# A step of the feed forward's norm one turn sooner: the last part of a four-layer gated transformer on one core

## The chip, the cores and the metric

One Trainium2 chip, one core of it. The metric is the device time of one execution in microseconds; the kernel before took 4783.49 us, the median of three runs (4782.34 to 4784.24).

## The reference

`x` holds 4 batches of 512 tokens with 256 features. Four layers of gated cross attention and feed forward follow each other, and the feed forward of the last layer is a transformer of its own, six deep. All that concerns us is inside it:

```python
def ffn_layer(x, g, bln, W1, b1, W2, b2):
    mu = x.mean(-1, keepdims=True)
    var = ((x - mu) ** 2).mean(-1, keepdims=True)
    xn = (x - mu) / jnp.sqrt(var + 1e-05) * g + bln
    hg = xn @ W1 + b1
    a, gate = jnp.split(hg, 2, -1)
    return a * jax.nn.gelu(gate, approximate=False) @ W2 + b2
for i in range(DEPTH):      # 6
    x = attn_layer(shift_tokens(x), Wqkv[i], q_scale[i], k_scale[i], Wo[i]) + x
    x = ffn_layer(shift_tokens(x), ln_g[i], ln_b[i], W1[i], b1[i], W2[i], b2[i]) + x
```

`attn_layer` is a local attention over windows of 64 tokens, 16 heads of 64 features. `shift_tokens` takes the second half of the features from the token before.

## The kernel before

The first part of the kernel (up to about 2124 us, where L1634 first runs) does everything but those six layers and isn't touched. The last part (`last_part`, L1276) works on transposed data, features in the partitions, in plain fp32 kept exact by splitting: each operand is a high part and a remainder (`xs_hi`, `xs_lo` and so on), and each product is three matmuls.

The order of the work is written out by hand. `last_order` (L1214) gives each stage of each unit a **turn**, sorts the stages of a turn by rank, and returns one list; every engine walks through the same list and issues its own share of each stage, in that order. A unit is a depth `d`, a quarter of the heads `g` and a batch `b`; it takes four turns, one per 128 tokens, so a depth has 64 turns and all six have 384. Turn numbers below are those inside a depth, 0 to 63, and batch 2's and 3's later steps fall in the next depth's first turns. In each turn, in this order:

- "sc": TensorE adds the window mask (L1511) and the scores (L1516); VectorE takes the row maxima (L1648) and combines them with the norms (L1652).
- "pv": TensorE multiplies with the values (L1535); ScalarE writes `att_hi` (L1777), VectorE the remainder (L1663).
- "tr": TensorE transposes queries and keys (L1501); ScalarE copies them out (L1752, L1757).
- "rot": POOL adds the two halves of the rotary product (L1818), takes the norm (L1820, L1822) and scales the keys (L1825); VectorE sums the squares for it (L1642).
- "dv", "ex": VectorE divides (L1657, L1659); ScalarE takes the exponentials (L1764).
- "pt": TensorE transposes the probabilities (L1525); ScalarE copies them out (L1770).
- "wx", in two of four turns: VectorE adds the output projection to the residual (L1670).
- then the feed forward's stages that have this turn, and "xs", the splitting of the next input (ScalarE L1735, POOL L1809).
- "qkv": TensorE projects (L1493, twelve matmuls); VectorE makes the rotary products (L1634, L1635, L1636); ScalarE copies the values (L1742) and squares (L1745), which frees the bank of queries and keys.
- "wo", in two of four turns: twelve matmuls of the output projection (L1449).
- "lq": a piece of weights: SyncE loads it, VectorE rounds it (L1618), POOL takes the remainder (L1814).

The feed forward of one batch, batches 0 and 2 ("even") from turn 32 of their half, batches 1 and 3 ("odd") from turn 49, has these steps:

- "fo": POOL adds the two halves of the features (L1830) into the buffer `n0`.
- "fa": TensorE multiplies with a matrix of 1/256 for the mean (L1556, two matmuls for the profile); VectorE subtracts it (L1676, twice) into `c0` and `c1`.
- "fq": ScalarE squares them (L1782, twice) into `n0` and `n1`; POOL adds (L1833).
- "fb": TensorE sums over the features (L1561); VectorE adds epsilon (L1680); POOL raises to the power -1/2 (L1836).
- "fy": TensorE spreads the result over the partitions (L1569); VectorE multiplies (L1685, twice).
- "fc": ScalarE adds the offset and rounds to `xn_hi` (L1790, twice).
- "fd": VectorE makes the remainder `xn_lo` (L1692, twice). The first gate product waits for it.
- "hg", three times: gate products (L1449, twelve matmuls) and ScalarE's gelu (L1798). "ha" and "hm", three times: linear products, VectorE's product of both (L1702), its rounding (L1709, L1712), POOL's remainder (L1842). The last "ha" and "hm" of a batch are in turn 50 (even) and 34 (odd, counted from the next half's start); so they fall one or two turns behind the next batch's "fo".
- "fw" and "fx": second product (L1449, L1596, L1597) in three parts, and VectorE's addition to the residual (L1717).

Memory is handed out by `plan` (L84) from the same list, when the program is built: a free slot is taken from the head of a queue and a freed one put at its end, so that the stage that opens a slot waits for the signal that freed it. Two of these queues matter here. `one` (L1360) deals out six PSUM banks. "qkv" takes two (freed by `sq_act`, that is L1745, and by L1742), "hg" two, and "fa", "fb", "fy", "tr", "pt", "pv" one each. `work_at` (L1402) deals out the nine buffers of `lwork`: "qkv" opens three (`sq`, `t1`, `t2`), "rot" frees `sq` and `t2` (the latter by POOL's L1825), "tr" three turns later frees `t1`; "fo" opens `n0`, "fa" `c0` and `c1`, "fq" `n1`; "fb" frees the two `n`, "fd" the two `c`; "hg" opens two for the gates, "hm" frees them (by POOL's L1842, the last by VectorE's L1712). VectorE waits for the buffers of `t1` and `t2` ahead of L1634.

```python
def plan(order, slots, opens, closes):
    free, held, got, turns = [(s, None) for s in slots], {}, {}, {}
    for p in order.parts:
        for key in opens(p):
            slot, before = free.pop(0)
            ...
        for key, signal in closes(p):
            free.append((held.pop(key), signal if isinstance(signal, tuple) else (signal, order.nth[p])))
```

Of the kernel before, what the change touches and what calls it, by code (L numbers as in the profile page):

```python
# [1213 lines left out]
def last_order():  # L1214


    turn = {}

    def put(t, *parts):
        turn.setdefault(t, []).extend(parts)  # L1220

    def load(t, step, name, chunks):
        for n, j in enumerate(chunks):
            put(t + n * step, ("lq", name + (j,)))

    halves = [((0, 0), (1, 0), (1, 1), (0, 1), (2, 0), (3, 0), (3, 1), (2, 1)), ((2, 2), (3, 2), (3, 3), (2, 3), (0, 2), (1, 2), (1, 3), (0, 3))]
    units = [(d, g, b) for d in range(DEPTH) for half in halves for g, b in half]
    for d in range(DEPTH):
        t0 = 64 * d
        for key, q, o in (((0, 0), -4, 5), ((0, 1), 0, 9), ((0, 2), 12, 21), ((0, 3), 16, 25), ((1, 0), 44, 53), ((1, 1), 48, 57)):  # L1230
            load(t0 + q if t0 + q >= 0 else -2, 1 if t0 + q >= 0 else 0, ("q", d) + key, range(3))
            load(t0 + o, 1, ("o", d) + key, range(1))
        for t, j in ((27, 0), (28, 3), (30, 1), (31, 4), (35, 2), (36, 5), (38, 6), (39, 7), (40, 8)):
            load(t0 + t, 0, ("f", d), [j])
        put(t0 - 44 if d else -1, ("rt", d))
        for b, t in enumerate((-3, 6, 29, 38)):
            put(t0 + t if d or b > 1 else -2, ("xs", (d, b)))
    for n, (d, g, b) in enumerate(units):
        for stage, lag in (("qkv", 0), ("mv", 1), ("rot", 1), ("tr", 3), ("sc", 4), ("ex", 4), ("dv", 5), ("pt", 6), ("pv", 7)):
            for tt in range(QT):  # L1240
                put(4 * n + tt + lag, (stage, (d, g, b, tt)))
        for half in range(2):
            put(4 * n + 10 + half, ("wo", (d, g, b, half)))
            put(4 * n + 11 + half, ("wx", (d, g, b, half)))
    for d in range(DEPTH):
        for b in range(B):
            t0 = 64 * d + 32 * (b // 2)
            norm = (32, 35, 36, 37, 38, 39, 39) if b % 2 == 0 else (49, 51, 52, 53, 54, 55, 55)
            gates, linear, second = ((40, 44, 48), (41, 45, 50), (49, 52, 53)) if b % 2 == 0 else ((56, 60, 64), (57, 61, 66), (65, 68, 69))
            if d == DEPTH - 1 and b == B - 2:  # L1250
                gates, linear, second = (40, 42, 44), (41, 43, 45), (46, 47, 48)
            elif d == DEPTH - 1 and b == B - 1:
                norm, gates, linear, second = (40, 41, 42, 43, 44, 46, 46), (47, 49, 51), (48, 50, 52), (53, 54, 55)
            for t, stage in zip(norm, ("fo", "fa", "fq", "fb", "fy", "fc", "fd")):
                put(t0 + t, (stage, (d, b)))
            for j in range(HT // 2):
                put(t0 + gates[j], ("hg", (d, b, j)))
                put(t0 + linear[j], ("ha", (d, b, j)), ("hm", (d, b, j)))
            for i, t in enumerate(second):
                put(t0 + t, ("fw", (d, b, i)), *([("fx", (d, b, i - 1))] if i else []))  # L1260
            if d == DEPTH - 1:
                put(t0 + second[0], ("kb", b))
                put(t0 + second[2] + 1, ("fin", b))
    rank = {st: i for i, st in enumerate(("mv", "sc", "pv", "tr", "rot", "dv", "ex", "pt", "wx", "fo"))}
    rank.update({"qkv": 30, "wo": 31, "lq": 32})

    def place(t, p):

        if t < 0:
            return 40 if p[0] not in rank else rank[p[0]]  # L1270
        return rank.get(p[0], 20)

    return Order(p for t in sorted(turn) for p in sorted(turn[t], key=lambda p: place(t, p)))


def last_part(nc, a, at, s):  # L1276
# [3 lines left out]
    vec, sm, psum, tokens = at.vec, at.sm, at.psum, at.tokens  # L1280
    ident, ident_b, ones_mean = at.ident, at.ident_b, at.ones_mean
    order = last_order()
    S_ = {name: s(name) for name in (
        "xs_act xs_pool lq_dve lq_pool rt_dve qk_pe qkv_pe sq_act qkv_act qkv_dve rot_dve rot_pool tr_pe tr_act sc_pe sc_dve ex_act "
# [793 lines left out]
```

How the kernel before makes its waits and increments, by code:

```python
    def wait_ge(self, sem, value):  # L105
        if self.met.get(sem.name, 0) < value:
            self.engine.wait_ge(sem, value)
            self.met[sem.name] = value
# [12 lines left out]
    def join(self):  # L121
        self.waits.wait_ge(self.sem, self.n)
# [295 lines left out]
        def left(got, key, waits):  # L418
            before = got[key][1]
            if before:
                waits.wait_ge(S_[before[0]], before[1])
# [3 lines left out]
        def pair_left(key, i):  # L426
            before = two[key][1]
            if before:
                before = first_half.get(before, before) if i == 0 else before
                PE.wait_ge(S_[before[0]], before[1])
# [25 lines left out]
        def tensor_program():  # L457
            for stage, u in order.walk():
                if stage == "ln1":
                    PE.wait_ge(S_["ln0_pool"], at_("ln0", u))
                    left(one, ("ln1", u), PE)
                    tensor.matmul(bank(("ln1", u)), ones_mean[:, :], buf(("ln", u, 0)), start=True, stop=True).then_inc(S_["ln1_pe"], 1)
                elif stage == "ln2":
                    PE.wait_ge(S_["ln1_pool"], at_("ls", u))
                    left(one, ("ln2", u), PE)
                    for tt in range(QT):
                        ins = tensor.matmul(bank(("ln2", u))[:, tt:tt + 1], buf(("ln", u, 0))[:, tt * P:(tt + 1) * P], ones_mean[:, 0:1],
# [1 line left out]
                    ins.then_inc(S_["ln2_pe"], 1)  # L469
                elif stage == "ln3":
                    PE.wait_ge(S_["ln2_pool"], at_("ln2", u))
                    left(one, ("ln3", u), PE)
```

## Time and profile before

| | |
|---|---|
| median of three runs | 4783.49 us |
| the profiled execution, and its span | 4783.06 us, 4781.7 us |
| TensorE matmul busy | 4568.2 us, 96% |
| VectorE busy | 3604.3 us, 75% |
| ScalarE busy | 3167.6 us, 66% |
| POOL busy | 2593.5 us, 54% (in the last part 8 tenths) |
| TensorE clock granted, mean | 0.989 |

The span is the time from the first to the last instruction of one profiled execution. Busy times of different engines overlap. The idle time of an engine before an instruction is put down to the event that ended it, its releaser; a wait of TensorE costs time, a wait of another engine only where TensorE waits for it in turn. In the chain of waits the profile goes back from the last instruction to what released each one.

### The profile page before, as it was taken

To read this page: it belongs to the slowest core of one execution; us is meant where nothing else is said; L and a number is where in the kernel's file an instruction comes from. 1 tells how busy PE (TensorE), PEld (TensorE's weight loads), DVE (VectorE), ACT (ScalarE), POOL (GpSimd) and SP (SyncE) were. 2 spreads that over 40 slices of the span, in tenths; PEclk is the share of its full clock that TensorE was granted. 3 is DMA by queue.
4 is the path that set the end of the run, shared out by engine and by line. 5 is a ranking of instruction groups with operands and counts; after the bars stand their busy time and mean duration, and the time that the engine had idled before them with its cause. 6 is when DMAs were issued, how large, how long until landed. Compare 5 with 4: busy or idle time off the path is not lost.

```text
span 4781.7 us, 94769 instructions
## 1 busy us (share of the span) xinstructions
PE 4568.2 (96%) x35816; PEld 3008.6 (63%) x35816; DVE 3604.3 (75%) x6388; ACT 3167.6 (66%) x7744; POOL 2593.5 (54%) x2346
## 2 busy tenths in 40 slices
PE   6999999999999899969999999999999999999998
PEld 2333333334444343338888888888888888888887
DVE  4777766766675857858888888888888788888885
ACT  3666566555555556547777777777777777777774
POOL 3222211212121222139888888787888888887873
PEclk8999999999999999989999999999999999999999
DMA  5323323332222323311111111111111111111111
GB/s 123 64 51 62 75 41 61 71 64 47 57 41 57 72 41 67 47 33 53 44 38 39 40 41 36 40 41 38 36 46 40 38 39 40 41 36 35 41 45 31
DMA packets 178934, 233.20 MB, mean 49 GB/s; under 512 B 29648, under 2 KB 121424, under 8 KB 178256
## 3 DMA queue, kind: packets, MB, share of 16 engines
q1 hardware_dynamic: 178480, 227.14, 20.9%
q8 instruction: 286, 4.69, 0.4%
q14 instruction: 168, 1.38, 0.1%
HBM read 150.09 MB, written 32.51 MB: 38 GB/s over the span
## 4 chain that ended last, share of the span: by engine, by line
PE 78%; DVE 10%; ACT 6%; issue 3%; POOL 2%; DMA 1%; SPq 0%; DVEq 0%; ACTq 0%; POOLq 0%
PE psum L1449 15%; PE psum L1493 14%; PE psum L541 5%; PE psum L527 5%; PE psum L506 5%; PE psum L1535 4%; PE psum L1501 4%; PE psum L1525 3%; PE psum L1516 3%; PE psum L488 2%; DVE maxes L731 2%; PE psum L530 2%; PE psum L1511 2%; PE psum L496 2%; DVE sums L764 1%
## 5 line engine op out<-in xcount | busy, mean ns | idle before, releaser
L941 ACT ACTIVATE probs<-psum 128x1024 f32<-128x1024 f32 x610 | 621.6, 1023 | 449.9 <-PE psum L527 259.7
L731 DVE TENSOR_REDUCE maxes<-psum 128x1 f32<-128x1024 f32 x512 | 618.1, 1216 | 276.9 <-PE psum L506 273.1
L1764 ACT ACTIVATE lprobs<-psum,small_stats,stats 128x128 f32<-128x128 f32 x1536 | 689.1, 477 | 22.7 <-DVE small_stats L1652 21.9
L1822 POOL TENSOR_TENSOR stats<-stats,minus_half 128x8 f32<-128x8 f32 x384 | 676.5, 1762 | 32.0
L1818 POOL TENSOR_TENSOR lwork<-lwork 128x512 f32<-128x512 f32 x384 | 510.4, 1329 | 108.3 <-DVE lwork L1636 106.6
L1493 PE MATMUL psum<-wqkv_hi,xs_hi 128*128 128x512 f32 (+1 forms) x1536 | 541.4, 352 | 16.4 <-POOL xs_lo L1809 15.6
L527 PE MATMUL psum<-stack 98*128 98x512 bf16 x1536 | 502.9, 384 | 22.9 <-DVE maxes L731 12.2
L1493 PE MATMUL psum<-wqkv_hi,xs_lo 128*128 128x512 f32 (+1 forms) x1536 | 518.5, 338 | 0.0
L1493 PE MATMUL psum<-wqkv_lo,xs_hi 128*128 128x512 f32 (+1 forms) x1536 | 518.5, 338 | 0.0
L506 PE MATMUL psum<-stack 96*128 96x512 bf16 x1536 | 472.1, 384 | 33.7 <-ACT probs L938 10.0
L728 DVE CUSTOM_DVE_ANT_0 psum<-psum,mask_by_query 128x1024 f32<-128x1024 f32 x256 | 314.8, 1231 | 217.8 <-PE psum L506 216.2
L1745 ACT ACTIVATE lwork<-psum 128x512 f32<-128x512 f32 x384 | 229.7, 598 | 325.6 <-DVE lwork L1636 322.0
L1634 DVE TENSOR_TENSOR lwork<-psum,rotary 128x512 f32<-128x512 f32 x384 | 262.8, 684 | 236.5 <-PE psum L1493 217.2
L541 PE MATMUL psum<-probs,values 128*32 128x512 f32 x3072 | 412.6, 609 | 0.8 <-ACT probs L941 0.8
L1659 DVE TENSOR_TENSOR lprobs<-lprobs,small_stats 128x512 f32<-128x512 f32 x384 | 384.3, 1001 | 13.1
L527 PEld LDWEIGHTS psum<-stack 98*128 98x128 bf16 x1536 | 137.9, 100 | 389.8 <-issue 219.2
L1764 ACT ACTIVATION_READ_ACCUMULATOR lprobs<-psum,small_stats,stats 128x1 f32 x1536 | 344.0, 224 | 0.0
L1089 POOL TENSOR_TENSOR attn<-attn,sums 128x512 f32<-128x512 f32 x48 | 62.2, 1296 | 502.6 <-DVE sums L764 502.6
L1493 PEld LDWEIGHTS psum<-wqkv_hi,xs_hi 128*128 128x128 f32 x1536 | 291.2, 190 | 64.4 <-issue 16.7
L1493 PEld LDWEIGHTS psum<-wqkv_lo,xs_hi 128*128 128x128 f32 x1536 | 291.5, 190 | 42.5 <-issue 1.4
L506 PEld LDWEIGHTS psum<-stack 96*128 96x128 bf16 x1536 | 147.5, 98 | 262.0 <-ACT probs L938 27.8
L1493 PEld LDWEIGHTS psum<-wqkv_hi,xs_lo 128*128 128x128 f32 x1536 | 290.7, 189 | 32.0
(244 smaller groups left out, 11838.6 us busy)
## 6 DMA issues: line engine op xcount, KB each, us to landing
mixed_vals<-vals SPq DMA_DIRECT2D x672, 64.0 KB, 2.0
stack<-k_parts SPq DMA_DIRECT2D x288, 128.0 KB
staged<-in_quads SPq DMA_DIRECT2D x144, 256.0 KB, 2.9
k_parts<-parts SPq DMA_DIRECT2D x48, 384.0 KB, 2.9
stack<-q_parts SPq DMA_DIRECT2D x288, 64.0 KB
staged<-in_w SPq DMA_DIRECT2D x54, 256.0 KB, 3.0
ctx<-in_ctxT SPq DMA_DIRECT2D x24, 512.0 KB, 5.1
q_parts<-parts SPq DMA_DIRECT2D x24, 384.0 KB, 3.2
```

Of the source, the lines that this page charges most:

```text
L506: ins = tensor.matmul(ps[:, i, :], q[0:STACK, h, qt * P:(qt + 1) * P], k[0:STACK, h, i * S:(i + 1) * S], start=True, stop=True)
L527: ins = tensor.matmul(ps[:, i, :], ky[0:STACK + 2, h, kt * P:(kt + 1) * P], q[0:STACK + 2, h, :], start=True, stop=L != 1)
L541: ins = tensor.matmul(bank(acc)[32 * h:32 * h + 32, :], values[:, kt, 4 * g + h, :], pr, start=kt == 0, stop=kt == KT - 1)
L728: ins = vector.tensor_tensor_reduce(out=scores, in0=scores, in1=masks_q[:, qt * S2:(qt + 1) * S2], scale=1.0, scalar=-3e38, op0=ALU.add, o ...
L731: ins = vector.tensor_reduce(to, pair(("M", u)), AX.XY, ALU.max)
L941: scalar.activation(probs[:, i % 6, :, :], pair(("E", u)), ACT.Exp).then_inc(S_["E_act"], 1)
L1449: ins = tensor.matmul(ps, l, r, start=first and n == 0, stop=last and n == 2)
L1493: ins = tensor.matmul(to, x_[:, c, b % 2, tok(tt)], w_[:, c * COLS + lo:c * COLS + hi], start=c == 0 and n == 0, stop=c == C - 1 and n == 2)
L1659: vector.tensor_tensor(pr, pr, bc(rc, 2, P), ALU.mult).then_inc(S_["dv_dve"], 1)
L1764: ins = scalar.activation(pr[:, h, :], scores(u)[:, h % 2, h // 2, :], ACT.Exp, bias=st[:, 4 + h:5 + h], scale=y[:, h:h + 1], accum_out=st ...
L1818: gpsimd.tensor_tensor(t1, t1, t2, ALU.add)
L1822: pool_step(gpsimd.tensor_tensor(st[:, 8:16], st[:, 0:8], minus_half[:, :], ALU.pow))
```

## The change

The feed forward's norm gets other turns, all but its first step. The seven numbers are those of "fo", "fa", "fq", "fb", "fy", "fc", "fd". "fa" to "fc" each come one turn sooner; "fd" keeps its turn, so that "fc" and "fd" no longer share one. The last batch of the last depth has turns of its own, which stay.

```diff
@@ last_order @@
         for b in range(B):
             t0 = 64 * d + 32 * (b // 2)
-            norm = (32, 35, 36, 37, 38, 39, 39) if b % 2 == 0 else (49, 51, 52, 53, 54, 55, 55)
+            norm = (32, 34, 35, 36, 37, 38, 39) if b % 2 == 0 else (49, 50, 51, 52, 53, 54, 55)
```

No instruction is added or left out. The queues of banks and buffers are dealt out anew from the new list.

## Rows read from the trace of the kernel before

**Rows 1.** The page: span, and busy time of TensorE (share of span, instructions)

```profile
span 4781.7 us, 94769 instructions
PE 4568.2 (96%) x35816; PEld 3008.6 (63%) x35816; DVE 3604.3 (75%) x6388; ACT 3167.6 (66%) x7744; POOL 2593.5 (54%) x2346
```

**Rows 2.** TensorE's waits after 2330 us: total us, times, longest us

```profile
PE psum L1449 <- ACT lwork L1745: 33.7, 22, 1.8
PE psum L1525 <- ACT lwork L1745: 7.1, 10, 1.1
```

**Rows 3.** VectorE's waits after 2330 us, same columns

```profile
DVE xn_lo L1692 <- ACT xn_hi L1790: 35.5, 23, 1.9
```

**Rows 4.** Timeline, turns 55 and 56: start us, us, instruction, [idle before <-releaser]

```profile
3314.47 0.68 DVE L1670 TENSOR_TENSOR x_resid<-psum,x_resid 128x512 f32<-128x512 f32 x1
...
3317.08 1.41 DVE L1692 SCALAR_TENSOR_TENSOR xn_lo<-lwork,vecs,xn_hi 128x512 fp32r<-128x512 f32 x2 [1.93 <-ACT xn_hi L1790]
...
3319.34 0.42 DVE L1636 TENSOR_TENSOR lwork<-psum,rotary 128x256 f32<-128x256 f32 x1
...
3319.79 0.60 ACT L1745 ACTIVATE lwork<-psum 128x512 f32<-128x512 f32 x1 [2.47 <-DVE lwork L1636]
...
3314.14 1.94 POOL L1822 TENSOR_TENSOR stats<-stats,minus_half 128x8 f32<-128x8 f32 x1
...
3316.74 0.30 PE L1511 MATMUL psum<-band_bias,ident_b 64*64 64x256 bf16 x4
...
3318.51 0.60 PE L1525 MATMUL psum<-ident,lprobs 128*128 128x128 f32 x4
3320.53 0.47 PE L1449 MATMUL psum<-xn_hi,w_hi 128*128 128x512 f32 x1 [1.42 <-ACT lwork L1745]
```

**Rows 5.** Chain that ended last, around 3285 us: the mean's two matmuls

```profile
3285.40 0.86 PE psum L1556 x2
```

**Rows 6.** Timeline, turns 50 to 52 of depth 2: TensorE, VectorE, then POOL

```profile
3275.57 0.30 PE L1511 MATMUL psum<-band_bias,ident_b 64*64 64x256 bf16 x4
...
3282.78 0.30 PE L1511 MATMUL psum<-band_bias,ident_b 64*64 64x256 bf16 x4
...
3284.77 0.63 PE L1525 MATMUL psum<-ident,lprobs 128*128 128x128 f32 x4
...
3289.73 0.30 PE L1511 MATMUL psum<-band_bias,ident_b 64*64 64x256 bf16 x4
...
3282.64 0.69 DVE L1634 TENSOR_TENSOR lwork<-psum,rotary 128x512 f32<-128x512 f32 x1
...
3283.58 0.41 DVE L1636 TENSOR_TENSOR lwork<-psum,rotary 128x256 f32<-128x256 f32 x1
...
3288.28 1.27 DVE L1676 TENSOR_TENSOR lwork<-x_resid,psum 128x512 f32<-128x512 f32 x2
...
3283.04 1.27 POOL L1842 TENSOR_TENSOR hid_lo<-lwork,hid_hi 128x512 fp32r<-128x512 f32 x1
3284.68 1.27 POOL L1814 TENSOR_TENSOR wqkv_lo<-staged,wqkv_hi 128x512 fp32r<-128x512 f32 x1 [0.36 <-DVE wqkv_hi L1618]
...
3289.68 0.61 POOL L1825 TENSOR_TENSOR lwork<-lwork,stats 128x256 f32<-128x256 f32 x1
```

**Rows 7.** Timeline, batch 0 of depth 2, turns 35, 38 and 40

```profile
3175.76 0.63 PE L1525 MATMUL psum<-ident,lprobs 128*128 128x128 f32 x4 [1.08 <-ACT lwork L1745]
...
3200.26 1.19 ACT L1735 ACTIVATE xs_hi<-x_resid 128x512 fp32r<-128x512 f32 x2
...
3207.28 1.67 POOL L1822 TENSOR_TENSOR stats<-stats,minus_half 128x8 f32<-128x8 f32 x1
...
3207.95 1.42 DVE L1692 SCALAR_TENSOR_TENSOR xn_lo<-lwork,vecs,xn_hi 128x512 fp32r<-128x512 f32 x2 [1.51 <-ACT xn_hi L1790]
```

**Rows 8.** Line L1634: its waits for POOL (us, times), and the longest, in depth 0

```profile
  POOL lwork L1825: 6.7, 4
...
2319.72 0.69 DVE L1634 TENSOR_TENSOR lwork<-psum,rotary 128x512 f32<-128x512 f32 x1 [2.60 <-POOL lwork L1825]
```

## The prediction

> **What bounds the kernel now.** I read the page first, then who waited for whom in the last part, then the order of time around two turns of one batch. The profiled span is 4781.7 us and TensorE is busy for 96% of it [rows 1]. So an edit of the order can give back only what TensorE waits for, and costs only where it adds to that. Of the waits of TensorE after 2330 us, two carry this change [rows 2]: the first gate product of a batch (stage "hg", L1449) waited 22 times, 33.7 us in total, for ScalarE's square L1745, and the transpose of the probabilities (stage "pt", L1525) waited 10 times, 7.1 us, for the same line. L1745 frees the PSUM bank that either of them takes.
>
> Who made L1745 late? [Rows 3] show it before the gate product: VectorE waited 23 times, 35.5 us, for ScalarE's L1790 ("fc"), the other half of the norm's end, in the turn of its own L1692 ("fd"). [Rows 4] are one such case, batch 1 of depth 2, turns 55 and 56. VectorE is free at 3314.47 + 0.68 = 3315.15, stands still for 1.93, and does the pair L1692 at 3317.08; behind it on the same queue stand the three rotary products that end with L1636 at 3319.76; then L1745 runs 3319.79 to 3320.39, and TensorE starts at 3320.53. Its transposes L1525 had started 1.77 after the turn's first instruction L1511, and take their four places in about 0.36, so it could have gone on at 3318.87: 1.66 us are lost.
>
> **What the change removes.** "fc" now runs one turn ahead of "fd". In turn 55 VectorE finds xn_hi ready and starts L1692 at 3315.15, 1.93 sooner; L1636 ends at 3317.83, L1745 at about 3318.5, and with the 0.14 from its end to TensorE's start the bank is free at 3318.6, before 3318.87. The wait goes whole: 1.66 us per batch. TensorE's own order is next, so no more than this can come.
>
> On the even batches (0 and 2) less comes. Their "fc" lands in turn 38 (6 for batch 2), where ScalarE also converts the next input (L1735, 1.19 us [rows 7]) ahead of it. L1742 and L1745 of that turn then start later by the two L1790 (taken as long as the two L1692, 1.41 [rows 4]), and the turn behind it gets its bank and its att_hi late. I follow this to about 0.2 us at the next turn's projection and 0.5 us at the gate product; I take 0.95 back on batch 0 and 1.2 on batch 2.
>
> **What it adds.** The other six steps move too. No instruction and no DMA is added or dropped; SyncE's queue is passed by none of them. "fa" (TensorE 0.86 [rows 5], then two subtractions L1676 on VectorE, 1.27 [rows 6]) goes from turn 51 to 50 (35 to 34). Turn 50 is the one in which the batch before has its last "ha" and "hm", so VectorE's longest turn gets 1.27 more. Two things follow from how the nine buffers of lwork are handed out: first freed, first taken, so the k-th opening takes the (k-9)-th closing.
>
> *Turn 50.* At "fa" five buffers are with the projection's pipeline, one is n0; c0 and c1 take the two oldest. The projection then takes what "rot" of this same turn freed (L1825) and, as its third, the one that "hm" of this same turn frees by POOL's L1842. Before, it took none of POOL's of that turn. [Rows 6]: turn 50 starts at 3275.57, turn 51 at 3282.78, turn 52 at 3289.73. With 0.86 of "fa" in it, turn 51 starts at 3283.64. VectorE has done "hm" by 3282.6, does L1676 until 3283.9, and waits for L1842, which ends at 3283.04 + 1.27 = 3284.31. So L1634 starts at 3284.4 and not at 3282.64: 1.76 later. L1636 ends at 3285.75, L1745 at 3286.4, and "pt" can start at 3286.55. Without a wait it would at 3283.64 + 1.77 = 3285.41: a wait of 1.13 where now there is 3284.77 - 3282.78 - 1.77 = 0.22. Turn 52 then starts at 3283.64 + 6.95 - 0.86 - 0.22 + 1.13 = 3290.64.
>
> *Turn 51.* "fq" opens n1 here, so all four buffers of the norm are out, and the projection's third buffer is the one freed by L1825 of the same turn. That happens now in turns 52 and 53, where POOL is ahead; it comes in turn 51, where it is behind. The POOL chain hangs on VectorE: L1814 (the weights' remainder, queued ahead of "rot") started 1.10 after L1636's start, and from it to the end of L1825 (3289.68 + 0.61 = 3290.29) POOL hardly pauses. All of it comes 1.76 later: 3292.05. L1634 of turn 51, which started before L1825, now waits for it, and VectorE's queue behind it too (L1636, "sc", "pv", "rot", "dv"): L1636 ends at 3293.45, L1745 at 3294.1, "pt" of turn 52 starts at 3294.25 and not at 3290.64 + 1.77 = 3292.41. A wait of 1.84. In turn 52 the second products (eleven matmuls and "fb") give VectorE and POOL the time to come level.
>
> So the odd batches pay 1.13 + 1.84 - 0.22 = 2.75 and get 1.66: +1.09 each. Bounds of the second wait: nothing, if "hm" finds POOL free and the 1.76 shrinks by what a shorter queue gives; and 2.6, which is the longest such wait that the trace has behind L1825 (four in all, 6.7 us [rows 8], so 1.7 in the mean). I take 1.84, next to that mean.
>
> *Even batches.* The pattern is the same, 16 turns earlier. In batch 0 the weights' pieces come in turns 35 and 36, so L1814 doesn't stand ahead of "rot" in 35, but "pt" of turn 35 waits already (1.08 idle, [rows 7]), since VectorE is late with "hm". The same working gives 1.4 idle in turn 35 and 0.6 in 36: +0.9 paid, 0.95 back. Batch 2 has the pieces where batch 1 has them: +2.7 paid, 1.2 back.
>
> "fq", "fb" and "fy" on TensorE and VectorE I cost at nothing: "fb" (0.8) and "fy" move into turns 52 and 53 beside "fw", as much as they leave in 53 and 54. What hides L1685 is that turn 53 has no residual addition; if that cover were gone it would cost at most its length, some 1.4 by the like pair L1692, per batch.
>
> **Sum.** Batch 3 of the last depth keeps its own turns, so 23 of 24 norms move. Eleven odd: 11 x 1.09 = +12.0. Batch 0, depths 1 to 5: 0. Batch 2, depths 0 to 4: 5 x 1.5 = +7.5. The first norm (no batch before it) and batch 2 of the last depth (nothing behind it to project): 0 within 2. Together +19 on the profiled execution's 4783.06, so 4802. The median of the runs is 4783.49, 0.4 above that execution, which changes nothing. About 0.2% (9.6 us) is what a measurement of this kernel can tell from no change.
>
> **A rule against the sum.** In turn 40 POOL's L1822 ran from 3207.28 to 3208.95, and VectorE's L1692, with two SBUF inputs, started in it at 3207.95 and took 0.71 each [rows 7]: no blocking. The Trainium skill, page "SBUF — State Buffer", section "Who interferes with whom", says that a VectorE instruction with two SBUF inputs and a GpSimd instruction that reads SBUF exclude each other for the whole of whichever came first. By that rule the sum would be higher, by the rival below.
>
> **Rivals.**
> 1. *The buffers don't bind.* VectorE and POOL catch up before L1634 of turn 51, only the first wait of 1.13 comes. For it: TensorE's extra 0.86 in turn 50 gives all of them time, and L1842 may start sooner. Against: POOL's chain in [rows 6] has no slack. Odd 1.13 - 0.22 - 1.66 = -0.75 each, -8; evens some -6 together: 4769. With neither wait it is 11 x 1.66 + 5 x 0.95 + 5 x 1.2 = 29 less: 4754. This is the one that ends faster; it decides where L1634 waits for L1825 by less than 0.75 us.
> 2. *It cancels.* The second wait is there at about half its size (0.9), and gain and cost meet: 4783 to 4790.
> 3. *Blocked halves.* L1692, now at 3315.15, meets L1822 (3314.14 to 3316.08, [rows 4]) and waits for its end, 0.93; 0.63 of the gain is lost in 21 batches: +13, 4815. This is what the rule above would do.
> That the steps don't move isn't open: the numbers are the turns.
>
> **Chances.** Forecast 0.52 (4793 to 4812), rival 3 0.05, rival 2 0.18, rival 1 0.25. Slower 0.57, within 0.2% 0.18, faster 0.25. The slower cases' own range is 4794 to 4816; to hold eight in ten the range must take in the part of rival 1 where the first wait comes: 4764 to 4816.
>
> **What would show it.** In the changed kernel's waits: VectorE for L1790 gone or nearly; L1449 behind L1745 from 33.7 to some 8 us, all on even batches; L1525 behind L1745 from 7.1 in 10 to 50 or 60 us in over 30; L1634 behind L1825 and L1842 some 40 times, up from 4. Turn 56 shorter by 1.7, turn 52 longer by 1.8 beyond the 0.8 of "fb". If L1634 doesn't wait for POOL in turn 51, my cost falls and it is rival 1. If "fc" in an even batch makes no late L1745, the evens gain more than I say.

## The result, and the profile after

| | before | after |
|---|---|---|
| median of five runs | 4783.6 us (4782.34 to 4786.46) | 4801.14 us (4800.99 to 4803.56) |
| the profiled execution, and its span | 4783.06, 4781.7 us | 4800.99, 4799.7 us |
| waits of VectorE's L1692 for L1790, after 2330 us | 35.5 us, 23 times | none |
| waits of TensorE's L1449 for L1745 | 33.7 us, 22 times | 7.4 us, 11 times |
| waits of TensorE's L1525 for L1745 | 7.1 us, 10 times | 49.9 us, 42 times |

The ratio of the times is 1.0038, with a 95% interval of 1.0025 to 1.0051: slower by 17.5 us, more than the 0.2% that a measurement of this kernel can tell. The forecast was 4802.

The page of the changed kernel, where [rows 1] have that of before:

```profile
PE 4567.6 (95%) x35816; PEld 3005.6 (63%) x35816; DVE 3595.2 (75%) x6388; ACT 3154.7 (66%) x7744; POOL 2600.3 (54%) x2346
...
PE 68%; POOL 10%; DVE 10%; ACT 6%; issue 4%; DMA 1%; SPq 0%; DVEq 0%; ACTq 0%; POOLq 0%
```

TensorE's busy time is the same to 0.6 us: all 18 us of span are waits. The last line is the chain that ended last. POOL had 2% of it before and has 10% now, so work of POOL has come onto the path.

Whom the waits name, TensorE first, then VectorE (total us, times, longest us, after 2330 us), against [rows 2, 3]:

```profile
PE psum L1525 <- ACT lwork L1745: 49.9, 42, 1.5
PE psum L1449 <- ACT lwork L1745: 7.4, 11, 0.9
...
DVE lwork L1634 <- POOL lwork L1825: 42.0, 21, 2.1
...
DVE lwork L1634 <- POOL hid_lo L1842: 8.5, 16, 0.5
```

The stall at the norm's end is gone, and with it 26 us of the gate product's wait. Two new rows of VectorE stand in its place, both of L1634 and both for POOL, and TensorE passes them on as waits of L1525. Read L1634's rows by their count: 21 waits for L1825 are 11 odd batches, 5 of batch 2 and 5 of batch 0; 16 waits for L1842 are the odd ones and batch 2.

The place where it happens is turns 50 to 52 of batch 1, depth 2, the turns of [rows 6]. TensorE, VectorE, ScalarE, then POOL:

```profile
3281.18 0.30 PE L1511 MATMUL psum<-band_bias,ident_b 64*64 64x256 bf16 x4
...
3289.27 0.30 PE L1511 MATMUL psum<-band_bias,ident_b 64*64 64x256 bf16 x4
...
3292.20 0.63 PE L1525 MATMUL psum<-ident,lprobs 128*128 128x128 f32 x4 [0.99 <-ACT lwork L1745]
...
3296.30 0.30 PE L1511 MATMUL psum<-band_bias,ident_b 64*64 64x256 bf16 x4
...
3299.72 0.63 PE L1525 MATMUL psum<-ident,lprobs 128*128 128x128 f32 x4 [1.48 <-ACT lwork L1745]
...
3288.26 1.29 DVE L1676 TENSOR_TENSOR lwork<-x_resid,psum 128x512 f32<-128x512 f32 x2
3290.07 0.69 DVE L1634 TENSOR_TENSOR lwork<-psum,rotary 128x512 f32<-128x512 f32 x1 [0.53 <-POOL hid_lo L1842]
...
3291.01 0.41 DVE L1636 TENSOR_TENSOR lwork<-psum,rotary 128x256 f32<-128x256 f32 x1
3291.34 0.42 DVE L1618 CAST wqkv_hi<-staged 128x512 fp32r<-128x512 f32 x1
...
3293.61 1.30 DVE L1659 TENSOR_TENSOR lprobs<-lprobs,small_stats 128x512 f32<-128x512 f32 x1
...
3297.59 0.69 DVE L1634 TENSOR_TENSOR lwork<-psum,rotary 128x512 f32<-128x512 f32 x1 [2.08 <-POOL lwork L1825]
...
3298.53 0.41 DVE L1636 TENSOR_TENSOR lwork<-psum,rotary 128x256 f32<-128x256 f32 x1
...
3298.98 0.60 ACT L1745 ACTIVATE lwork<-psum 128x512 f32<-128x512 f32 x1 [2.48 <-DVE lwork L1636]
...
3288.67 1.27 POOL L1842 TENSOR_TENSOR hid_lo<-lwork,hid_hi 128x512 fp32r<-128x512 f32 x1
3291.84 1.28 POOL L1814 TENSOR_TENSOR wqkv_lo<-staged,wqkv_hi 128x512 fp32r<-128x512 f32 x1 [1.90 <-DVE wqkv_hi L1618]
3293.07 1.29 POOL L1818 TENSOR_TENSOR lwork<-lwork 128x512 f32<-128x512 f32 x1
...
3296.85 0.62 POOL L1825 TENSOR_TENSOR lwork<-lwork,stats 128x256 f32<-128x256 f32 x1
```

In turn 50 VectorE would be ready for L1634 at 3289.5, but its buffer is still read by POOL's L1842 until 3289.94. That makes everything behind it late, POOL's next turn too: L1814 can't start before the cast L1618 that stands behind L1636 on VectorE, and POOL stands idle for 1.90. In turn 51 the same L1634 then needs the buffer of this turn's L1825, which ends at 3297.47, and waits 2.08. ScalarE's L1745 follows each L1636 within 0.1, and TensorE starts 0.14 after each L1745's end. The chain crosses four engines, and its cause, the handing out of buffers, appears in no row by its own name.

And the place where the change gives time back, turns 55 and 56, the turns of [rows 4]:

```profile
3322.64 0.68 DVE L1670 TENSOR_TENSOR x_resid<-psum,x_resid 128x512 f32<-128x512 f32 x1
3323.24 1.40 DVE L1692 SCALAR_TENSOR_TENSOR xn_lo<-lwork,vecs,xn_hi 128x512 fp32r<-128x512 f32 x2
...
3322.31 1.93 POOL L1822 TENSOR_TENSOR stats<-stats,minus_half 128x8 f32<-128x8 f32 x1
...
3325.93 0.60 ACT L1745 ACTIVATE lwork<-psum 128x512 f32<-128x512 f32 x1 [1.66 <-DVE lwork L1636]
...
3324.91 0.30 PE L1511 MATMUL psum<-band_bias,ident_b 64*64 64x256 bf16 x4
...
3327.04 0.48 PE L1449 MATMUL psum<-xn_hi,w_hi 128*128 128x512 f32 x1
```

L1692 starts as L1670 ends, and L1449 starts 2.13 after its turn's L1511, where it was 3.79 before: 1.66 back. L1745 still ends at 3326.53, half a microsecond before the bank is wanted.

A turn is the stretch from its first L1511 to the next turn's. The seven turns from "fa" to the first gate product, depth 2, before and after (read from the starts of L1511, in us):

| turn of an odd batch | 50 | 51 | 52 | 53 | 54 | 55 | 56 | sum |
|---|---|---|---|---|---|---|---|---|
| batch 1 before | 7.21 | 6.95 | 7.03 | 7.83 | 6.29 | 5.85 | 8.77 | 49.93 |
| batch 1 after | 8.09 | 7.03 | 9.52 | 7.38 | 5.86 | 5.85 | 7.13 | 50.86 |
| batch 0 before (34 to 40) | 7.21 | 7.96 | 6.93 | 7.83 | 6.29 | 5.85 | 8.77 | 50.84 |
| batch 0 after | 8.09 | 7.43 | 8.50 | 7.38 | 5.86 | 5.89 | 7.83 | 50.98 |
| batch 2 before (2 to 8) | 7.21 | 7.25 | 7.05 | 7.83 | 6.29 | 5.85 | 9.12 | 50.60 |
| batch 2 after | 8.09 | 7.27 | 9.54 | 7.38 | 5.86 | 5.89 | 8.25 | 52.28 |

Batch 2's turns 2 to 8 are those of depth 3. Its turn 8 took 10.72 in the kernel before, in a stretch of a lower clock (last section); the table has the 9.12 of other depths in its place, and the sum with that.

So an odd batch loses 0.93, batch 0 loses 0.14, batch 2 loses 1.68. Eleven, five and five of them make 10.2 + 0.7 + 8.4 = 19.3, and the span grew by 18.0. The lower clock cost the kernel before 1.6, which brings 19.3 to 17.7. The rest lies outside the table: the changed kernel is about 1.2 shorter before and between these turns, mostly in depth 0, and 1.45 longer behind the last turn, where its own clock fell twice.

### The profile page after: what moved, and what is told of

Its sections match the earlier page's. It is cut to its first block, busy times and chain, and to the rows that moved or that the text cites. A ratio compares the mean times of both kernels' runs of the same rounds, so it can differ in the third digit from the quotient of the medians.

```text
span 4799.7 us, 94728 instructions
## 1 busy us (share of the span) xinstructions
PE 4567.6 (95%) x35816; PEld 3005.6 (63%) x35816; DVE 3595.2 (75%) x6388; ACT 3154.7 (66%) x7744; POOL 2600.3 (54%) x2346
## 4 chain that ended last, share of the span: by engine, by line
PE 68%; POOL 10%; DVE 10%; ACT 6%; issue 4%; DMA 1%; SPq 0%; DVEq 0%; ACTq 0%; POOLq 0%
PE psum L1449 13%; PE psum L1493 12%; PE psum L541 5%; PE psum L527 5%; PE psum L506 5%; PE psum L1535 3%; PE psum L1501 3%; POOL stats L1822 3%; PE psum L1525 2%; PE psum L488 2%; DVE maxes L731 2%; PE psum L1516 2%; PE psum L530 2%; POOL lwork L1818 2%; PE psum L496 2%
## 5 line engine op out<-in xcount | busy, mean ns | idle before, releaser
L1822 POOL TENSOR_TENSOR stats<-stats,minus_half 128x8 f32<-128x8 f32 x384 | 680.3, 1772 | 32.0
L1818 POOL TENSOR_TENSOR lwork<-lwork 128x512 f32<-128x512 f32 x384 | 511.8, 1333 | 100.3 <-DVE lwork L1636 99.8
L1634 DVE TENSOR_TENSOR lwork<-psum,rotary 128x512 f32<-128x512 f32 x384 | 262.8, 684 | 267.1 <-PE psum L1493 199.0
L1745 ACT ACTIVATE lwork<-psum 128x512 f32<-128x512 f32 x384 | 230.7, 601 | 327.4 <-DVE lwork L1636 323.3
L1659 DVE TENSOR_TENSOR lprobs<-lprobs,small_stats 128x512 f32<-128x512 f32 x384 | 387.6, 1009 | 13.1
L1648 DVE TENSOR_REDUCE psum<-psum 128x4 f32<-128x512 f32 x384 | 265.8, 692 | 62.5 <-PE psum L1516 59.5
```

Of the source, the lines that this page charges most:

```text
L1659: vector.tensor_tensor(pr, pr, bc(rc, 2, P), ALU.mult).then_inc(S_["dv_dve"], 1)
L1818: gpsimd.tensor_tensor(t1, t1, t2, ALU.add)
L1822: pool_step(gpsimd.tensor_tensor(st[:, 8:16], st[:, 0:8], minus_half[:, :], ALU.pow))
```

## The experiments

Two theories of why the change costs time were to be told apart. Mine: the early "fa" and "fq" hold buffers of lwork that the projection then has to take fresh from POOL; the split of "fc" and "fd" is a pure gain. The rival: the early steps cost by the work that they add to turns 50 and 51 (VectorE's longest turns, or POOL's), whatever buffers there are. The kernels of the first four experiments shared one set of runs of the kernel before (median 4783.28), the other four another (4784.29). Diffs are against the changed kernel.

### The split alone

"fa" and "fq" go back to their old turns. "fb" and "fy" too; "fc" stays one turn ahead of "fd", and "fy" shares its turn.

```diff
-            norm = (32, 34, 35, 36, 37, 38, 39) if b % 2 == 0 else (49, 50, 51, 52, 53, 54, 55)
+            norm = (32, 35, 36, 37, 38, 38, 39) if b % 2 == 0 else (49, 51, 52, 53, 54, 54, 55)
```

> Only the end of the norm is split: 'fc' comes one turn sooner, in the turn of 'fy', and everything before it keeps its turn. My theory (the gate product waits because VectorE stands still for 'fc' in the turn of 'fd'; the slowdown comes from 'fa' and 'fq' coming sooner, and not from this part): 1.66 us less for each of 11 odd batches, 0.9 for 10 even ones, where ScalarE's L1735 stands ahead of 'fc', so some 27 less than before: 4757. TensorE's waits behind L1745 fall from 33.7 to some 9 us for L1449 and stay at 7 for L1525. Rival A (ScalarE can't hold 'fc' one turn sooner, since it now waits for 'fy' of the same turn and L1742 and L1745 stand behind it): half of it or less, 4770 or more. Rival B (it is the sooner 'fc' that made the changed kernel slower): 4795 to 4810.

Measured: 4751.63 us (4747.66 to 4754.24), ratio to before 0.9929 (0.9917 to 0.9942). TensorE's waits for L1745 and VectorE's for L1790:

```profile
PE psum L1525 <- ACT lwork L1745: 7.1, 10, 1.1
PE psum L1449 <- ACT lwork L1745: 3.1, 11, 0.3
...
DVE xn_lo L1692 <- ACT xn_hi L1790: 0.8, 1, 0.8
```

The wait of L1525 is the 7.1 us of before to the tenth, that of L1449 fell by 30.6 us, and the time fell by 31.7. Half of the diff is a gain of 0.7%.

### The early steps alone

The other half: "fa" to "fy" early as in the change, "fc" and "fd" together in one turn.

```diff
-            norm = (32, 34, 35, 36, 37, 38, 39) if b % 2 == 0 else (49, 50, 51, 52, 53, 54, 55)
+            norm = (32, 34, 35, 36, 37, 39, 39) if b % 2 == 0 else (49, 50, 51, 52, 53, 55, 55)
```

> 'fa', 'fq', 'fb' and 'fy' one turn sooner, 'fc' stays in the turn of 'fd'. It leaves out what pays and keeps what costs. My theory: the changed kernel's 4801 plus what the split gives back, some 27: 4828, with waits of L1525 behind L1745 of about 50 us and of L1449 behind L1745 of about 34 us. Rival B (the cost lies in the sooner 'fc'): 4784.

Measured: 4829.84 us (4825.63 to 4830.12), ratio 1.0092 (1.0078 to 1.0106). The same two rows of TensorE, and the two of VectorE:

```profile
PE psum L1525 <- ACT lwork L1745: 50.1, 42, 1.5
PE psum L1449 <- ACT lwork L1745: 31.6, 22, 1.9
...
DVE lwork L1634 <- POOL lwork L1825: 41.9, 21, 2.1
DVE xn_lo L1692 <- ACT xn_hi L1790: 37.0, 22, 1.9
```

This kernel has both stalls: that of before at L1449 and that of after at L1525. The two halves give +46.6 and -31.7, together +14.9, and the change with both gives +17.5. The halves add to within 3 us, less than the interval of either; they act at different turns.

### The odd batches alone

The even batches keep the turns of before.

```diff
-            norm = (32, 34, 35, 36, 37, 38, 39) if b % 2 == 0 else (49, 50, 51, 52, 53, 54, 55)
+            norm = (32, 35, 36, 37, 38, 39, 39) if b % 2 == 0 else (49, 50, 51, 52, 53, 54, 55)
```

> The new turns for the odd batches alone. By the turns of the two traces an odd batch loses 0.93 us from its turn 50 to 56, so 11 of them 10: 4794. If the batches work on each other over the turns between them, it is not half and half: anywhere from 4784 to 4801.

Measured: 4794.31 us (4791.48 to 4798.03, eleven runs), ratio 1.002 (1.0011 to 1.0029): +11.0, so 1.0 per odd batch, and 6.5 of the 17.5 are the even ones.

```profile
PE psum L1525 <- ACT lwork L1745: 33.7, 31, 1.9
...
DVE lwork L1634 <- POOL lwork L1825: 22.8, 11, 2.1
```

Eleven waits of L1634 for L1825, one for each odd batch whose steps moved, of 2.07 each.

### The change with two more buffers

The changed kernel with eleven buffers of lwork in place of nine. Memory for them comes from `x_back`, which is laid on the rotary table's first slot, which is read for the last time in depth 4; SyncE waits for that reader before it loads there.

```diff
-        work = psb("lwork", [P, 9, S])
+        work = psb("lwork", [P, 11, S])
...
-        back = psb("x_back", [P, C, S])
+        back = rotary[:, 0].rearrange("p a t j d -> p (a t j d)").rearrange("p (c n) -> p c n", c=C)
...
-        work_at = plan(order, range(9), work_opens, work_closes)
+        work_at = plan(order, range(11), work_opens, work_closes)
...
+                    SP.wait_ge(S_["qkv_dve"], at_("qkv", (DEPTH - 2, 0, B - 1, QT - 1)))
```

> The changed kernel with eleven buffers of lwork in place of nine (the room is taken from x_back, which lies on the rotary table's half of the depth before). My theory (the second wait is the buffer that POOL's L1825 of the same turn frees): L1634 no longer waits for POOL, the second wait of 1.65 goes, the first shrinks from 1.16 to some 0.6: odd batches 0.6 - 0.22 - 1.66 = -1.3 against before, batch 0 -0.7, batch 2 -0.8; 4783 - 22 = 4761. Rival (VectorE and POOL just have too much in turns 50 and 51, whoever waits for whom): 4795 to 4801, with the waits of TensorE's L1525 where they are.

Measured: 4759.25 us (4756.34 to 4761.97), ratio 0.9945 (0.9932 to 0.9959). Not one step of the order differs from the changed kernel, and it is 41.9 us faster than that. L1634 no longer waits for POOL after 2330 us; TensorE's rows are

```profile
PE psum L1525 <- ACT lwork L1745: 14.3, 21, 1.3
PE psum L1449 <- ACT lwork L1745: 8.1, 11, 1.4
```

and turns 50 and 51 of the same batch, TensorE in turn 51, then VectorE and POOL in both:

```profile
3275.53 0.30 PE L1511 MATMUL psum<-band_bias,ident_b 64*64 64x256 bf16 x4
...
3277.85 0.63 PE L1525 MATMUL psum<-ident,lprobs 128*128 128x128 f32 x4 [0.37 <-ACT lwork L1745]
...
3275.73 0.68 DVE L1634 TENSOR_TENSOR lwork<-psum,rotary 128x512 f32<-128x512 f32 x1
...
3281.09 0.68 DVE L1634 TENSOR_TENSOR lwork<-psum,rotary 128x512 f32<-128x512 f32 x1
...
3274.93 1.29 POOL L1842 TENSOR_TENSOR hid_lo<-lwork,hid_hi 128x512 fp32r<-128x512 f32 x1
...
3282.49 0.61 POOL L1825 TENSOR_TENSOR lwork<-lwork,stats 128x256 f32<-128x256 f32 x1
```

Both L1634 start while POOL is still busy with what freed their buffer in the changed kernel: the one of turn 50 at 3275.73 inside L1842 (to 3276.22), the one of turn 51 1.4 before L1825. POOL comes to L1842 as late as in the changed kernel (7.49 after the turn's first L1511 in both) and to L1825 0.62 sooner (6.96 and 7.58), since the L1634 ahead of it didn't wait; but nobody waits for either. This is the experiment that decides between the theories: the rival has the same work in the same turns and should have stayed near 4800. What remains to it is small. The wait at L1525 of turn 51 is 3277.85 - 3275.53 - 1.77 = 0.55, where the split alone has 0.22 there. The 0.33 between them is what the rival is right about: the work of "fa" on VectorE's longest turn. And 4759.25 is 7.6 above the split alone.

### "fa" early, the rest as in the split alone

Which of the two early openings costs what? Here "fa" comes in turn 50, "fq" in 52, so the fourth buffer isn't out in turn 51.

```diff
-            norm = (32, 34, 35, 36, 37, 38, 39) if b % 2 == 0 else (49, 50, 51, 52, 53, 54, 55)
+            norm = (32, 34, 36, 37, 38, 38, 39) if b % 2 == 0 else (49, 50, 52, 53, 54, 54, 55)
```

> Of the early steps 'fa' alone: it comes one turn sooner, 'fq', 'fb' and 'fy' keep their turns, and the end is split as in the run that split it alone (4751.6). n1 is then opened a turn later than in the changed kernel, and the projection of turn 51 takes no buffer from POOL. My theory (the first wait is VectorE's 'hm' and 'fa' in one turn, the second is the buffer of n1): only the first wait comes, 0.9 more for 16 batches and next to nothing for batch 0: 4751.6 + 15 = 4767, with L1634 behind L1825 in the last part only in depth 0. Rival (the second wait comes from VectorE and POOL being late, whatever the buffers): 4785 or more, with turn 52 about as long as in the changed kernel.

Measured: 4769.24 us (4766.78 to 4770.48), ratio 0.9967 (0.9954 to 0.9979). TensorE and VectorE:

```profile
PE psum L1525 <- ACT lwork L1745: 24.2, 21, 1.8
...
DVE lwork L1634 <- POOL hid_lo L1842: 8.4, 16, 0.5
```

L1842's row of the changed kernel is back (8.4 in 16), L1825's is not. In turn 51 the wait is 3279.14 - 3276.22 - 1.77 = 1.15:

```profile
3276.22 0.30 PE L1511 MATMUL psum<-band_bias,ident_b 64*64 64x256 bf16 x4
...
3279.14 0.63 PE L1525 MATMUL psum<-ident,lprobs 128*128 128x128 f32 x4 [0.98 <-ACT lwork L1745]
```

The time is the 4767 of the theory, within its interval, and not the 4785 of the rival. So "fa" one turn sooner makes the first wait and costs 17.6 us over the split alone. "fq" one turn sooner, with "fb" and "fy" behind it, makes the second and costs another 31.9 up to the changed kernel.

### The kernel before with eleven buffers

The control: does the kernel before gain from the buffers too? Its turns, and the edits of the eleven buffers as above.

```diff
-            norm = (32, 34, 35, 36, 37, 38, 39) if b % 2 == 0 else (49, 50, 51, 52, 53, 54, 55)
+            norm = (32, 35, 36, 37, 38, 39, 39) if b % 2 == 0 else (49, 51, 52, 53, 54, 55, 55)
...
-        work = psb("lwork", [P, 9, S])
+        work = psb("lwork", [P, 11, S])
```

> The control: the kernel before with eleven buffers of lwork, made room for in the same way. If the extra buffers only cure what the change brought, nothing but the few waits for POOL in depth 0 (6.7 us, 4 times) can go: 4776 to 4783. If they are worth something by themselves (so that the changed kernel's gain from them says nothing about the change): under 4770.

Measured: 4781.74 us (4779.4 to 4785.56, eleven runs), ratio 0.9995 (0.9986 to 1.0004): no change that can be told. Two buffers are worth 42 us to the changed kernel and about nothing to the one before. The lack of buffers was made by the change.

### The next input's splitting away from "fc"

The split alone left 3.1 us at L1449, all on even batches, where ScalarE's L1735 ("xs") shares the turn of "fc". Here "xs" of two of the four batches comes one turn sooner, and every "xs" stands behind the feed forward's stages of its turn. "xs" is ScalarE's L1735 and POOL's L1809, so both move.

```diff
-        for b, t in enumerate((-3, 6, 29, 38)):
+        for b, t in enumerate((-3, 5, 29, 37)):
...
-            norm = (32, 34, 35, 36, 37, 38, 39) if b % 2 == 0 else (49, 50, 51, 52, 53, 54, 55)
+            norm = (32, 35, 36, 37, 38, 38, 39) if b % 2 == 0 else (49, 51, 52, 53, 54, 54, 55)
...
-        return rank.get(p[0], 20)
+        return 25 if p[0] == "xs" else rank.get(p[0], 20)
```

> The split end of the norm, and the next input's splitting (ScalarE L1735, POOL L1809) one turn sooner for batches 1 and 3 and behind the feed forward's steps in its turn, so that it no longer shares a turn with 'fc' of an even batch. My theory (L1735 ahead of 'fc' is why the even batches got less): their rest wait of 0.5 at the gate product goes, 10 times: 4751.6 - 5 = 4746 or 4747. Rival (the rest comes from 'fc' waiting for 'fy' in its own turn): 4751 to 4755, since L1735 now only crowds turn 37.

Measured: 4747.22 us (4746.2 to 4747.69), ratio 0.9921 (0.9908 to 0.9935), 4.4 below the split alone in median. Their intervals overlap, but the trace shows where it comes from: of L1449's eleven waits one of 0.4 us is left, turn 40 is 7.14 (7.63 with the split alone) and turn 8 is 7.31 (7.67). In five depths each that is 0.49 x 5 + 0.36 x 5 = 4.2, and the spans differ by 3.9.

The number is the forecast one, but the traces show another cause than the theory's. They are VectorE's product L1659 in turn 7 of depth 3 (batch 2), with the split alone and then here:

```profile
3407.90 1.46 DVE L1659 TENSOR_TENSOR lprobs<-lprobs,small_stats 128x512 f32<-128x512 f32 x1
...
3407.60 0.70 DVE L1659 TENSOR_TENSOR lprobs<-lprobs,small_stats 128x512 f32<-128x512 f32 x1
```

With the split alone POOL's L1809 stands ahead of its L1818, which then runs from 3407.52 to 3408.82, beside L1659. Here L1818 is over at 3406.66. ScalarE's share went the other way: VectorE waits 0.36 for `att_hi` (0.27 with the split alone) and starts L1659 9.80 after turn 6's start, not 9.40; only the product's shorter time brings the next L1692 forward, 11.03 for 11.39. In turn 39 of batch 0 it is L1692 itself that took 1.83 beside L1818 and takes 1.40 here, and ScalarE's L1790 had been done for 3.7 us. So what the run gave back is time that VectorE lost beside POOL, whose L1818 was late behind L1809. No run moved L1735 without L1809.

### The same with eleven buffers

```diff
-        work = psb("lwork", [P, 9, S])
+        work = psb("lwork", [P, 11, S])
```

> The same with eleven buffers: the sum of the two, so what the control gains from them (0 to 5) less than the run before: 4741 to 4746. If the buffers' waits of depth 0 are covered there by something else, 4746.

Measured: 4745.3 us (4741.39 to 4747.48), ratio 0.9917 (0.9903 to 0.993). It is the fastest here, by 1.9 us in median over the one before it, which the intervals don't tell apart. Of the table's turns, turn 3 of depth 3 is 6.70 instead of 7.21 and the turn behind it 6.93 instead of 7.02; the others of that depth and of depth 2 are the same within 0.03. Both beat the kernel before by 0.8% and the changed one by 1.1% or more. They are what the experiments recommend, and the version with nine buffers has them in four numbers and a rank.

## Why the prediction was right

**The stall removed.** Predicted: L1692 starts when L1670 ends, 1.66 us per odd batch. L1692 waits for nothing, L1449 starts 1.66 sooner, and turn 56 is 1.64 shorter. The split alone shows the step by itself: -31.7 against the 29 that the prediction has for neither wait (11 x 1.66, 5 x 0.95, 5 x 1.2).

**The first wait** (turn 51, for L1842 of turn 50). Predicted 1.13, measured 3292.20 - 3289.27 - 1.77 = 1.16. L1634 was to wait until L1842's end and 0.1 more, and did (3289.94, 3290.07). Turn 51 was to start 8.07 after turn 50; it did after 8.09.

**The second wait** (turn 52, for L1825 of turn 51). Predicted 1.84, measured 3299.72 - 3296.30 - 1.77 = 1.65. This is the term that was mis-sized. The step that failed a little is "All of it comes 1.76 later". The chain of POOL was hung on L1636 with the distance of before, 1.10 from L1636's start to L1814's; now it is 3291.84 - 3291.01 = 0.83. Between them stands the cast L1618, which takes 0.42 now that POOL stands idle, and in the kernel before took 0.69, while POOL's L1842 ran:

```profile
3283.91 0.69 DVE L1618 CAST wqkv_hi<-staged 128x512 fp32r<-128x512 f32 x1
```

The lateness itself had moved the cast out from beside POOL's work, and so took back some of what it cost: 0.27 of it, of which 0.08 went again in steps that came a little later than forecast, so that L1825 ended 0.19 before its forecast time.

**"fb", "fy", "fq" at nothing.** Turns 52, 53 and 54 together grew by 22.76 - 21.15 = 1.61 us, no more than the second wait. So the moved products and L1685 cost nothing, as costed.

**Odd batches.** Predicted 2.75 paid, 1.66 back, +1.09 each; measured +0.93 in the turns, +1.0 in the experiment with them alone.

**Batch 0.** Predicted 0 (0.9 paid, 0.95 back), measured +0.14: turns 34 to 38 grew by 1.03, turn 40 shrank by 0.94, turn 39 grew by 0.04. The two waits are there as told: L1525 starts 1.57 and 0.63 late in turns 35 and 36 (1.25 and 0.01 before).

**Batch 2.** Predicted +1.5 (2.7 paid, 1.2 back), measured +1.68 (2.51 paid in turns 2 to 6, 0.04 in turn 7, 0.87 back in turn 8). The gain was taken too large. Turn 7 shows why beside turn 55, which has the same steps. VectorE waits 0.71 for `att_hi`, 0.11 in turn 55: that is the conversion L1735 and the two L1790 on ScalarE, as the prediction followed them. But then the product L1659 takes 1.64 beside POOL's L1818, late behind L1809, where it takes 0.70 in turn 55. VectorE and POOL in turn 7, then VectorE in turn 55:

```profile
3432.82 1.64 DVE L1659 TENSOR_TENSOR lprobs<-lprobs,small_stats 128x512 f32<-128x512 f32 x1
...
3432.62 1.30 POOL L1818 TENSOR_TENSOR lwork<-lwork 128x512 f32<-128x512 f32 x1
...
3322.01 0.70 DVE L1659 TENSOR_TENSOR lprobs<-lprobs,small_stats 128x512 f32<-128x512 f32 x1
```

These 0.94 are in no term of the prediction. The kernel before had them too (1.62 in that turn), but there they only shortened VectorE's wait for L1790, from 1.93 to 1.02.

The two misses, 11 x 0.16 too much and 5 x 0.14 + 5 x 0.18 too little, nearly cancel, and so the total is better than its parts. That is luck.

**Rival 1, the buffers don't bind,** named the world in which the change is a gain, 4754 to 4769. It falls for this kernel, L1634 waited 2.08 for L1825 and not under 0.75. But the kernel with eleven buffers is just that world, at 4759.25, between the two figures. With the quarter that I gave it, the sign hung on one question, whether POOL has slack in turn 51; the rows said no.

**Rival 2, it cancels,** wanted a second wait of half the size, 0.9: it was 1.65.

**Rival 3, blocked halves.** It wanted L1692 to wait for L1822's end in 21 batches. L1822 ran from 3322.31 to 3324.24, the two L1692 from 3323.24 to 3324.64, 0.70 each: no blocking, as in [rows 7]. But on batch 0, in all six depths, the first L1692 meets POOL's L1818 instead, and the pair takes 1.84 in place of 1.40:

```profile
3213.18 1.84 DVE L1692 SCALAR_TENSOR_TENSOR xn_lo<-lwork,vecs,xn_hi 128x512 fp32r<-128x512 f32 x2
...
3212.06 1.74 POOL L1818 TENSOR_TENSOR lwork<-lwork 128x512 f32<-128x512 f32 x1
```

This 0.44 is part of what keeps turn 40 at 7.83, where turn 56 is 7.13. So the rival had a real mechanism and the wrong instruction for it. The rule of the Trainium skill, page "SBUF — State Buffer", section "Who interferes with whom", by which two such instructions exclude each other, does not show against POOL's power on 128x8. Against POOL's wide instructions the trace agrees with it. The product L1659, two SBUF inputs, took 1.30 in turn 51: L1818 had 0.75 left as it started (3293.07 to 3294.36). In the whole trace of the changed kernel L1659 started 222 times inside one 128x512 instruction of POOL with over 0.2 us of it left, up to 1.24, and each time it took that rest and 0.54 to 0.56. It waits the rest out in full; with a sharing the time would grow by less than the rest. Why the power doesn't block is not shown.

**The counts** foretold were L1525 waiting over 30 times, 50 to 60 us (42 and 49.9), L1634 some 40 times for POOL (37), L1449 with some 8 us on even batches alone (7.4 in 11).

## What to carry to other kernels

A step moved ahead in a hand-written order holds its buffers longer, and where buffers go round first freed, first taken, some other stage then gets one that is freed in the same turn by a slower engine. So list, for the turns that the step newly covers, which release each opening takes, and when that engine gets there. The sign of the wait shows one engine over: a row of waits on a third engine's line, with a buffer as its object, where the work between the two has nothing to do with each other. And split a change that moves several steps: here one half gained 32 us and the other lost 47. Where a run's number comes out as forecast, look in its trace for the cause all the same: moving "xs" gave the forecast 4 us, by POOL's half of the stage and, as far as the two traces show, not by ScalarE's.

## What the hardware showed

**The clock fell behind one wait, and not behind others like it.** Turn 8 of depth 3 took 10.72 us in the kernel before, and 9.12 to 9.16 in the other four depths. A window of that turn shows why (stretch, length, then busy us of PE, PEld, DVE, ACT and POOL with their counts, the granted clock, the DMA share, GB/s):

```profile
3430.50:3432.00 1.50, 1.50 (x5) 1.12 (x5) 1.47 (x4) 1.50 (x8) 0.72 (x3) 0.50 0.00 0
```

TensorE had stood still for 1.78 behind L1745, and as it went on the granted clock was 0.50, the lower level of 1.2 GHz, for some 3 us; its matmuls took 0.63 each in place of 0.39, and the turn 1.6 longer. The other waits of this length in this kernel had no such stretch, so it is not the length alone. The kernel with the early steps alone had one too, behind a wait of 1.88 in turn 40 of depth 0 (10.85 us instead of 8.8), the control with eleven buffers one behind 1.77 in turn 8 of depth 2 (10.74), and the odd batches alone one behind L1525's wait of 1.86 in turn 51 of depth 5 (granted 0.50 from 4611.0 to 4614.3). The changed kernel has none in its turns, but two behind its last turn: 0.50 from 4726.7 to 4730.0, after 2.90 of idle time, and from 4757.4 to 4760.7. The kernel before has 1.00 there, from 4690 to 4780. One such stretch cost the kernel before 1.6 us, 0.03% of its time, and only some of the like waits have one behind them; what decides which isn't shown.

**A cast beside POOL.** L1618 took 0.42 with POOL idle and 0.69 with the last 0.40 of POOL's L1842 beside it, the same instruction in the same turn of the two kernels. It has one SBUF input and waits like the product above: in the changed kernel 56 of these casts started inside one 128x512 instruction of POOL with over 0.2 left, and took the rest of it and 0.28 or 0.29. It was this that made the second wait shorter than forecast.
